# Parts of q and k sent from SBUF straight into the operand stack, x taken by halves, and the last units sent by the next stage

## The reference

```python
x  = L0_attn_x                                  # [1, 1024, 256]
xn = layernorm(x)
s  = differential_attention(xn, Wq, Wk, Wv, Wo, lambdas, gn_w, gn_b)  # 16 heads, 4 k/v heads, 2 maps each, rope, causal
g  = silu(mxfp4_linear(xn, weight, bias))
x  = x + s * g
xn = layernorm(x)
s  = causal_attention(xn, Wq, Wk, Wv, Wo, bo)   # 16 heads of 16
g  = silu(moe(xn, gate_w, W1, W2, W3, Ws1, Ws2, Ws3))  # 16 experts, 4 chosen, one shared
x  = x + s * g                                  # the output
```

## Time and profile before

| | us |
|---|---|
| median of 3 runs | 868.28 |
| lowest, highest | 868.22, 869.21 |
| the profiled execution, its own time | 868.93 |
| its span, first to last instruction | 867.2 |

### The profile page before, as it was taken

The page is one execution under the profiler, slowest core; times in us unless marked ns, Lnnn a source line. Parts: engine busy times, 40 slices in busy tenths (PEclk is TensorE's granted clock), DMA queues, the critical chain, the costliest instruction groups (busy, mean ns, idle before and its releaser), DMA issues. The chain is left out here.

```text
span 867.2 us, 12855 instructions
## 1 busy us (share of the span) xinstructions
PE 762.9 (88%) x3632; PEld 365.0 (42%) x3632; DVE 529.4 (61%) x1441; ACT 432.3 (50%) x922; POOL 430.6 (50%) x751
## 2 busy tenths in 40 slices
PE   3938999999999999965984889999669999999995
PEld 2322222222222223222651222322148888888884
DVE  3649787778777768223653867886035555555555
ACT  1431666666666556732141256666534555455552
POOL 1751566654244324321222123334276999799994
PEclk9985999999999999975996698999969999999997
DMA  5393630110020011012059552432221212122221
GB/s 182 130 299 87 154 87 15 43 43 14 20 63 15 21 40 38 21 44 60 1 179 261 129 141 66 126 98 69 87 87 43 66 60 67 52 62 71 62 64 55
DMA packets 60075, 69.83 MB, mean 81 GB/s; under 512 B 14904, under 2 KB 40857, under 8 KB 60010
## 3 DMA queue, kind: packets, MB, share of 16 engines
q1 hardware_dynamic: 60016, 69.15, 28.4%
HBM read 47.35 MB, written 15.47 MB: 72 GB/s over the span
## 5 line engine op out<-in xcount | busy, mean ns | idle before, releaser
L675 ACT ACTIVATE top<-ps 128x512 f32<-128x512 f32 (+3 forms) x384 | 171.0, 490 | 132.4 <-PE ps L622 132.2
L605 PE MATMUL ps<-mid 96*128 96x512 bf16 (+3 forms) x576 | 191.2, 356 | 29.0 <-PEq L981 11.8
L709 DVE CUSTOM_DVE_ANT_0 ps<-ps,keep 128x512 f32<-128x512 f32 (+3 forms) x384 | 184.2, 504 | 41.9 <-PE ps L605 41.2
L622 PE MATMUL ps<-mid 99*128 99x512 bf16 (+3 forms) x576 | 185.7, 338 | 9.2 <-ACT mid L675 6.3
L1450 PE MATMUL ps<-xp,wp 128*128 128x512 f32 (+1 forms) x600 | 149.6, 400 | 14.3 <-ACT wp L1502 8.8
L642 PE MATMUL ps<-top,mid 128*33 128x512 f32 (+3 forms) x768 | 161.6, 500 | 0.0
L622 PEld LDWEIGHTS ps<-mid 99*128 99x128 bf16 x576 | 54.3, 99 | 185.8 <-ACT top L675 103.0
L1450 PEld LDWEIGHTS ps<-xp,wp 128*128 128x128 f32 (+1 forms) x600 | 115.0, 192 | 40.3 <-ACT xp L1504 9.3
L791 POOL TENSOR_SCALAR_AFFINE_SELECT top<-top 128x128 f32<-128x128 f32 x256 | 71.5, 294 | 109.4 <-ACT top L675 107.0
L675 ACT ACTIVATE mid<-ps 128x512 f32<-128x512 f32 (+1 forms) x192 | 82.6, 492 | 69.9 <-PE ps L622 41.8
L713 DVE TENSOR_REDUCE top<-ps 128x1 f32<-128x512 f32 x128 | 88.4, 691 | 36.0 <-PE ps L605 35.5
(11 more groups left out here) (199 smaller groups left out, 777.7 us busy)
## 6 DMA issues: line engine op xcount, KB each, us to landing
mid<-part_scratch SPq DMA_DIRECT2D x9, 1152.0 KB, 8.6
part_scratch<-top SPq DMA_DIRECT2D x18, 384.0 KB, 5.1
top<-in_w SPq DMA_DIRECT2D x16, 396.0 KB, 4.0
cw_s<-combine_rows SPq DMA_DIRECT2D x48, 128.0 KB, 3.0
part_scratch<-top SPq DMA_DIRECT2D x18, 256.0 KB, 5.2
mid<-part_scratch SPq DMA_DIRECT2D x9, 384.0 KB, 3.9
top<-inverse_scratch SPq DMA_DIRECT2D x12, 256.0 KB
top<-in_w SPq DMA_DIRECT2D x8, 384.0 KB, 5.4
```

Source lines behind the costliest of these rows:

```text
L605: nc.tensor.matmul(ps[:, s_bank(turn), 0:w], queries(pair, m)[0:PARTS, i * P:(i + 1) * P], keys(pair, m)[0:PARTS, c * 512:c * 512 + w], st ...
L622: nc.tensor.matmul(ps[:, ST_BANK + n % AHEAD, 0:w], keys(pair, m)[0:STACK, j * P:(j + 1) * P], queries(pair, m)[0:STACK, q0:q0 + w], start ...
L675: nc.scalar.activation(pr[:, n % RING, 0:w], ps[:, ST_BANK + n % AHEAD, 0:w], ACT.Exp, scale=0.25).then_inc(p_ready, 1)
L709: ins = nc.vector.tensor_tensor_reduce(bank, bank, msk[:, 512 - w:512], -1.0 if low else 1.0, 3e38 if low else -3e38, ALU.add, ALU.min if ...
```

## The change

1. **The way into the stack.** The DRAM tensors and the gathers are gone. `written` now sends each of the six part rows of a unit from `spl` directly into 16 partitions of the stack, all eight maps at once: six DMAs of 128 KB for a unit, in place of three and the gathers' share. So that one DMA can do this, the columns of q and k within a unit are in the order (element, map): `regrouped`, a copy on POOL, reorders the weights once (five copies of 256 elements a partition in layer 0, four in layer 1), `rope` is loaded as 16 rows, each to 8 partitions, and `swp` is made from the identity by two DVE copies.
2. **x by halves.** x comes in four DMAs, and statistics and 1/sqrt go by halves of it (the normalisation waits for both halves' statistics, and for each half's 1/sqrt); the identity is issued after the second DMA, the loads of rope go ahead of `wv`, and lambda's sum moves into the loop over units (u = 4).
3. **The order of units** in layer 0 is now (4,0), (0,0), (4,1), (0,1), then f = 1, 2, 3.
4. **The last units** (2 of 10 in layer 0, 4 of 8 in layer 1) are made in their stage but sent by attention's SP list (`early0`, `early1`), which then waits until every unit has landed and only then goes on to `rows(0)`. PE waits at pairs 0, 4, 8, 12 (in layer 1 at 0 and 4) for the units it needs.

```diff
-        def written(sp, to, f, c, parts, is_key, done):
-            rows = to[f * P:(f + 1) * P, :, c * 512:(c + 1) * 512]
-            for first_row, width, part in ((0, 3, 0), (3, 2, 1), (5, 1, 2)):
...
-                sp.dma_start(rows[:, first_row:first_row + width, :], of).then_inc(done, 16)
+        UN = [(4, 0), (0, 0), (4, 1), (0, 1)] + [(f, c) for f in (1, 2, 3) for c in range(NC)]
+        SENT = 8
+        def written(sp, stack, at, c, parts, is_key, done):
+            for n, part in enumerate(KPARTS if is_key else QPARTS):
+                sp.dma_start(stack[16 * n:16 * n + 16, at:at + 8, c * 512:(c + 1) * 512], parts[:, part, :]).then_inc(done, 16)
+        def by_row(w):
+            return w.rearrange("p k (m r) -> p k r m", r=16)
+        def regrouped(pool, to, of, f, done):
+            cols = slice(f * P, (f + 1) * P)
+            nc.gpsimd.tensor_copy(to[:, :, cols].rearrange("p k (r m) -> p k r m", r=16), by_row(of[:, :, cols])).then_inc(done, 1)
...
-                    for u, (f, c) in enumerate(UN):
+                    for u, (f, c) in enumerate(UN[0:SENT]):
                         sp.wait_ge(lo_ok, u + 1)
-                        written(sp, scr, f, c, spl[:, u % SLOTS, :, :], f == 4, scr_ok[u % SLOTS])
-                        if u == 2:
-                            near_maps0(sp, 4)
-                        if u == 3:
-                            near_maps0(sp, 0)
-                            far_maps0(sp, 0)
+                        written(sp, stack0, at0(f), c, spl[:, u % SLOTS, :, :], f == 4, scr_ok[u % SLOTS])
...
+                    for c in range(NC):
+                        four = slice(4 * c, 4 * c + 4)
+                        pool.wait_ge(stats, 4 * c + 4)
+                        link(nc.gpsimd.tensor_scalar(ve[:, four], mv[:, four, 1], EPS, None, ALU.add))
+                        nc.gpsimd.tensor_tensor(rst[:, four], ve[:, four], mhalf[:, four], ALU.pow).then_inc(rstd, 1)
+                    pool.wait_ge(ld_wk, 16)
+                    regrouped(pool, wk_s, wk_raw, 0, v_clr)
+                    pool.wait_ge(ld_wq, 16)
+                    for f in range(4):
+                        regrouped(pool, wq_s, qf, f, v_clr)
...
+        def early0(sp):
+            for u in range(SENT, len(UN)):
+                f, c = UN[u]
+                written(sp, stack0, at0(f), c, spl[:, u % SLOTS, :, :], f == 4, scr_ok[u % SLOTS])
+            for f in range(4):
+                wait_written(sp, 0, f)
...
+        def early1(sp):
+            for u, parts in left:
+                f, c = UN1[u]
+                written(sp, stack1, 8 * f, c, parts, f >= 2, scr_ok[u % SLOTS])
+            sp.wait_ge(comb_kept, 16)
+            for f in range(4):
+                wait_written(sp, 1, f)
```

More of the change, by code:

```diff
@@ L164, in unit_written @@
             before = len(range(slot, len(UN), SLOTS)) if layer == 1 else 0
-            return scr_ok[slot], 48 * (before + v // SLOTS + 1)
-        UN = [(f, c) for f in (4, 0, 1, 2, 3) for c in range(NC)]
+            return scr_ok[slot], 96 * (before + v // SLOTS + 1)
+        UN = [(4, 0), (0, 0), (4, 1), (0, 1)] + [(f, c) for f in (1, 2, 3) for c in range(NC)]
+        SENT = 8
         UN1 = [(2, 0), (0, 0), (2, 1), (0, 1), (3, 0), (1, 0), (3, 1), (1, 1)]
-        def written(sp, to, f, c, parts, is_key, done):
-            rows = to[f * P:(f + 1) * P, :, c * 512:(c + 1) * 512]
-            for first_row, width, part in ((0, 3, 0), (3, 2, 1), (5, 1, 2)):
[L174 to L177, removed]
-                sp.dma_start(rows[:, first_row:first_row + width, :], of).then_inc(done, 16)
@@ L220, in program @@
             le = sb("le", [P, 2], F32)
-            ld_x, ld_w, ld_c, ld_f, ld_r = (sem(n, a) for n in ("ld_x", "ld_w", "ld_c", "ld_f", "ld_r"))
+            ld_x = [sem(f"ld_x{n}", a) for n in range(4)]
+            ld_wk, ld_wq, ld_wv, ld_i, ld_c, ld_f, ld_r, ld_l = (
+                sem(n, a) for n in ("ld_wk", "ld_wq", "ld_wv", "ld_i", "ld_c", "ld_f", "ld_r", "ld_l"))
             stats, rstd, normed, ids = (sem(n, a) for n in ("stats", "rstd", "normed", "ids"))
@@ L323, in _ @@
[L323 to L326, removed]
-                    dve.wait_ge(rstd, 1)
-                    for t in range(NT):
+                    for odd in range(2):
+                        nc.vector.tensor_copy(turned(swp)[:, :, odd, :], turned(idf)[:, :, 1 - odd, :]).then_inc(ids, 1)
+                    for c in range(NC):
+                        for t in range(4 * c, 4 * c + 4):
+                            if t % 2 == 0:
+                                dve.wait_ge(ld_x[t // 2], 16)
+                            last = nc.vector.bn_stats(st6[:, t, :], xs[:, t, :])
+                        link(last)
+                        for t in range(4 * c, 4 * c + 4):
+                            nc.vector.bn_aggr(mv[:, t, :], st6[:, t, :]).then_inc(stats, 1)
@@ L329, in _ @@
+                    dve.wait_ge(stats, NT)
+                    for t in range(NT):
+                        if t % 4 == 0:
+                            dve.wait_ge(rstd, t // 4 + 1)
                         nc.vector.tensor_scalar(xn[:, t, :], xs[:, t, :], mv[:, t, 0:1], rst[:, t:t + 1],
                                                 ALU.subtract, ALU.mult).then_inc(normed, 1)
-                    dve.wait_ge(ld_r, 80)
-                    for n in range(2):
-                        last = nc.vector.tensor_tensor(lp[:, n, :], lm[:, 2 * n, :], lm[:, 2 * n + 1, :], ALU.mult)
@@ L334, in _ @@
-                    link(last)
-                    nc.vector.tensor_reduce(ls[:, :], lp[:, :, :], AX.X, ALU.add).then_inc(lsum, 1)
+                    nc.vector.memset(msk[:, 0:384], 0.0)
+                    dve.wait_ge(ld_c, 16)
+                    nc.vector.tensor_copy(msk[:, 384:512], tri[:, :])
+                    dve.wait_ge(ld_r, 32)
                     nc.vector.memset(lamv[:, 0:1], 1.0)
@@ L347, in _ @@
                                                     rp[:, 1, c * 512:(c + 1) * 512], ALU.mult).then_inc(roped, 1)
+                        if u == 4:
+                            dve.wait_ge(ld_l, 64)
+                            for n in range(2):
+                                last = nc.vector.tensor_tensor(lp[:, n, :], lm[:, 2 * n, :], lm[:, 2 * n + 1, :], ALU.mult)
+                            link(last)
+                            nc.vector.tensor_reduce(ls[:, :], lp[:, :, :], AX.X, ALU.add).then_inc(lsum, 1)
                         if u >= 1:
@@ L393, in _, with attention @@
                             last.then_inc(v_mm, 1)
-        def attention(layer, stack, vall, N, loaded, late):
+        def attention(layer, stack, vall, N, loaded, early):
             first = layer == 0
@@ L848, in ahead @@
                             rows(pair)
-                            late(sp, pair)
                             if not first:
                                 weights(pair)
+                        early(sp)
                         ahead(0)
@@ L978, in middle @@
         UN, scr_ok, unit_written, unit_near = (env[n] for n in ("UN1", "scr_ok", "unit_written", "unit_near"))
-        written, near_maps1, far_maps1 = env["written"], env["near_maps1"], env["far_maps1"]
-        EARLY = 4
+        written = env["written"]
+        for u in range(EARLY, len(UN)):
+            env["left"].append((u, spl[:, u % SPL, :, :]))
         with nc.Block() as block:
@@ L1011, in _ @@
                 link(nc.gpsimd.memset(mh4[:, :], -0.5))
+                pool.wait_ge(ldw, 64)
+                for f in range(4):
+                    env["regrouped"](pool, wqk, r1, f, v_clr)
                 pool.wait_ge(stats, 3)
```

114 lines of the change are left out of this document (40 added, 74 removed).

## The result

| | before | after |
|---|---|---|
| median of the runs compared, us | 868.25 | 883.29 |
| lowest, highest | 867.93, 869.21 | 882.69, 884.23 |
| span of the profiled execution | 867.2 | 881.5 |

The change makes the kernel slower: the ratio is 1.0172, 95% interval 1.0155 to 1.019. The forecast was 856, faster than before, with a range of 846 to 880, so both the sign and the range were wrong. The spans differ by 14.3 us.

The account below looks back on a forecast made before the run. Barriers held by SP's queued sends (6.7 and 9.1 us lost) and ACT's 2.48 us wait were taken to bound the kernel. Terms -4.9, -5.9 and -2.0 sum to -12.8 from 868.93: 856.1, median 855.5, stated as 856; range 846 to 880.

Parts of the forecast that it names:

- the price of a send: Sends of both projection stages: SP issues one per 0.63 us, 3.8 us a unit; bounds 0.52 and 0.88.
- rival A: Sends to the stack: 16 partitions are a narrow target, 1.3 us per 128 KB, 906 us median; chance 0.23.
- The second argument: Against rival A: the traced 32 KB copy is so short that a staggered start explains much of its 0.325 us.
- The formula: Net time change at d us a send, from both layers' rows(0) and attention's -2.0; zero at 0.85 us.
- Start of layer 0: Layer 0's start: x by halves makes the first projection and all that follows 4.3 us earlier, 13.8 for 18.15.
- Sends of layer 0: First barrier: sends end at 58.2, PE starts at 58.8 for 63.72, new wait covered by 4.6 us; -4.9 us.
- Sends of layer 1: Second barrier: PE starts 8.8 us earlier, but 24 issues ahead of rows(0) make SP 2.9 late; net -5.9 us.
- Attention: Attention 1: without gathers behind rows(1), ACT's 2.48 us wait for outputs shrinks; -2.0 us, bounds 0 and 2.5.
- B: Sends overlap only just, 0.75 to 0.85 us each; wait ahead of rows(0) eats the gain; 860 to 868; chance 0.17.
- C: SP's issues are cheap, 0.52 us each, and computing sets the projection stage's end; 847 us; chance 0.10.
- D: The change moves nothing, since the barrier's end is not what delays rows(0); chance 0.02.

Follow-up runs that it names:

- experiment 1: Changed kernel with each 128 KB send going to every sixth partition instead of 16 neighbours; 857.66 us, ratio 0.9907 to the kernel before.
- experiment 2: Changed kernel with each send going to 32 neighbouring partitions and four maps, rows misplaced; 868.94 us, ratio 1.001 to the kernel before.
- experiment 3: Changed kernel with each of a unit's six sends spread over partitions 0 to 95, wrong rows; 857.79 us, ratio 0.9907 to the kernel before.
- experiment 10: Changed kernel, layer 0's first 48 sends going eight in a row to the same 16 partitions, PE waiting for all 48; 897.37 us in one run.
- experiment 11: experiment 9 with targets of 16 neighbouring partitions again, ACT's queue sending its six in the order 3, 4, 5, 0, 1, 2; 875.39 us, ratio 1.0096.
- experiment 5: Kernel before with only x in two halves, and statistics, 1/sqrt and normalisation by halves; 863.33 us, ratio 0.9959.
- experiment 4: Changed kernel with SP's wait for all units moved behind rows(0) in both layers; 879.40 us, ratio 1.0159 to the kernel before.
- experiment 7: Changed kernel with sends to every sixth partition and SP's wait for all units behind rows(0); 855.83 us, ratio 0.9859 to the kernel before.
- experiment 8: experiment 1 with every unit sent in its own stage, none left to the next; 872.98 us, ratio 1.0049 to the kernel before.
- experiment 9: experiment 7 with four units left over in layer 0, and two of each layer's four left sent by ACT's queue; 846.03 us, ratio 0.9742.
- experiment 6: Kernel before with gathers and expert weights issued behind outputs(pair, 0) instead of ahead of it; 863.84 us, ratio 0.9953.

## Why the prediction was wrong

**The step that failed** is the price of a send: "The new ones are copies within SBUF: 0.63, 3.8 us a unit". It was the pace of SP's issues of 2 KB copies, and bounded by 0.88; a send took 1.02 us, outside the bounds of the sum. This is rival A's mechanism at a smaller size than its 1.3: shown by experiments 1, 2, 3 and 10, in which the changed kernel's sends differ only in where they land (in 3 also in how the bytes are shared among the six, and 10 has one more wait). The Trainium skill, page "SBUF — State Buffer", section "Door 1: The DMA port swizzle", gives 104 GB/s for 16 neighbouring partitions; experiment 10 agrees with it (105 to 112), and the changed kernel, which goes to another group each time, lies above it (128).

**Where I judged wrongly.** Against A I held that "successive sends go to different partitions and can run beside each other, which halves 1.3 to 0.65". Going to another group with every send wins 0.2 us (1.02 for 1.17 to 1.25), not 0.65. Two queues come to 166 GB/s in layer 0 and 127 in layer 1 (experiment 11). The section "Can I just issue two DMAs to hit both halves?" of the same page of the Trainium skill, which says that they hardly add up, stands nearer to this than my argument: the second queue added 25 to 37% in layer 0, by the windows with one queue (121 to 133), and nothing in layer 1. The second argument, the staggered start in the earlier trace rows, falls with experiment 10.

**The formula gives the time, but not by its terms.** With d = 1.02 it gives 28.0 + 61.2 + 1.7 - 77.88 = 13.0, and 461.7 + 24.5 + 1.7 - 484.66 = 3.2, less 2.0: +14.2, for 14.3 measured. Experiment 2 lies near its zero. That it comes so close is luck: by the marks, layer 0 came out 1.5 us above its term, layer 1 with the way there 3.8 above (7.7 - 0.75 - 3.2) and attention 1 5.2 below, which cancels.

**Term by term.** *Start of layer 0*, -4.3: met by experiment 5, with the transposes at 10.45 and the first projection at 13.89, where the prediction said 10.35 and 13.8, but -2.5 in the changed kernel's profile. In the ten profiles that have its start (the changed kernel and experiments 1 to 4 and 7 to 11) the statistics begin between 4.84 and 6.46 us, where 5.5 was estimated, and the projection 8.8 to 9.4 us behind them, where the prediction has 8.3. POOL's regrouping took 0.62 us a copy (3.12 for five), for 0.63 estimated, and hid. *Sends of layer 0*, -4.9 at rows(0), the start's share included, and 4.6 us of cover for the new wait: +14.55, and no cover. With sends of 0.67 us (experiment 1) PE starts at 62.15, rows(0) goes at 76.38 and the wait is covered. So even with a wide target the term would have been -1.5: 0.67 us a send for 0.63, and a first send 1.5 us later than the 28.0 said. *Sends of layer 1*, -5.9: +7.7. The wait ahead of rows(0) was foreseen; not foreseen was that the sends would hold the ring (ACT's 4.92 us) and PE's first scores (8.60 us). The 14.2 us ahead of either `rows(0)` hold, but what DVE reduces in them are the 24 blocks of pair 0 and the first few behind, not all 38; no term hangs on it. *Attention*, -2.0: -7.2, since "The clock is 0.50 in the first 19 us behind the barrier and I expect no other" left out the two stretches at 0.90 and 0.84; experiment 6 shows that the stall brings them.

**The rivals.** B's price for 0.85 is what experiment 2 measured. C's state, a stage bound by computing at 847, is not had from cheap issues; wide targets, a second queue, more units left over and rows(0) first together reach it, at 846.03, with 5.9 us saved in attention 1 where the sum for 847 has 2.5. D has nothing for it: moving the barrier moved rows(0) by as much in experiments 1, 8 and 9.

**Open.** Why two queues to different groups reach 166 GB/s in one layer and 127 in the other, and no more, was not taken further. That the DMA engines stand full at 1.15 in all the narrow cases fits engines that are held by a slow target and so can't serve another, but they are as full (1.14) at 212 GB/s with two queues and wide targets, and no run separates this from other causes.

## What to carry to other kernels

Before a DMA within SBUF replaces a way through DRAM, count the partitions on which one transfer lands, and price it by the slowest row of that shape, even if the row is a small one; a target of the same number of partitions spread over the whole range costs nothing more and was worth some 25 us here. Where a queue is full, moving a wait or an issue in the code gains little (2.0 of 9.4 us here); shorten the queue first, then move the wait. Where a stage ends in issues of one engine, leave the last to the next stage and share them with an idle engine's queue.

## What was not expected of the hardware

A stall of 2.48 us of ACT, and with it PE, cost 5.65 us, since the granted clock of PE, 1.00 with the stall away (experiment 6), is 0.90 and 0.84 in the stretches around it and behind it.

SP's issues within SBUF took 0.67 us each in a row of 60 of 128 KB (40.44 us, experiment 1), for 0.63 between 2 KB copies. The rate by the partitions of one send in SP's queue was 105 to 112 GB/s (16, the same ones again), 128 to 133 (16, others each time), 147 to 154 (32, the same ones twice in a row), and at least 197, the pace of SP's issues, with 16 partitions six apart, where a second queue brought it to 212.
